# Layer normalisations inside the stages that follow them, and a mixture of experts in one block

## The reference

```python
def _layernorm(x, axis=-1, eps=1e-05):
    m = jnp.mean(x, axis=axis, keepdims=True)
    v = jnp.var(x, axis=axis, keepdims=True)
    return (x - m) / jnp.sqrt(v + eps)
...
    x = x + _L1_xattn_ref(_layernorm(x, axis=-1), ctx_2048, ctx_2048, L1_xattn_gamma)
    x = x + _L1_ffn_ref(_layernorm(x, axis=-1), ...)
    x = x + _L2_attn_ref(_layernorm(x, axis=-1), ...)
    x = x + _L2_xattn_ref(_layernorm(x, axis=-1), ctx_2048)
    x = x + _L2_ffn_ref(_layernorm(x, axis=-1), ...)
    x = x + _L3_attn_ref(_layernorm(x, axis=-1), ...)
    x = x + _L3_xattn_ref(4, 256, 256, L3_xattn_w, L3_xattn_u, _layernorm(x, axis=-1), ctx_2048)
    x = x + _L3_ffn_ref(_layernorm(x, axis=-1), ...)
```

## Time and profile before

| | us |
|---|---|
| median of 3 runs | 1465.18 |
| lowest and highest run | 1462.57, 1465.30 |
| profiled execution: its time | 1461.6 |
| profiled execution: its span, first to last instruction | 1459.9 |
| TensorE busy in the span | 1221.0 (84%) |
| VectorE, ScalarE, GpSimd busy | 794.9, 510.2, 319.6 |
| mean granted TensorE clock | 0.893 of full speed |

### The profile page before, as it was taken

One profiled execution on the slowest core, in us unless ns is written; L12 is line 12 of the kernel. 1 busy time (PEld: TensorE's weight loads), 2 busy tenths in 40 slices (PEclk: granted clock), 3 DMA queues, 4 the chain that ended last, 5 costly groups with the idle time before them and its releaser, 6 DMA issues. The chain is left out here.

```text
span 1459.9 us, 22518 instructions
## 1 busy us (share of the span) xinstructions
PE 1221.0 (84%) x8843; PEld 755.3 (52%) x8850; DVE 794.9 (54%) x2082; ACT 510.2 (35%) x934; POOL 319.6 (22%) x351
## 2 busy tenths in 40 slices
PE   3768679797958799779995997999999978985597
PEld 1335464465734554456663554555555545653354
DVE  2886757207577444657865665343111135767944
ACT  1018325313515433445444455111111114445443
POOL 0215402200002200135540221232222213440000
PEclk9878879898969599879996997999999987897799
DMA  9000000000040020000000000123233200000000
GB/s 367 1 0 2 1 1 2 0 0 1 0 188 1 8 109 0 1 1 3 3 2 0 2 2 1 49 62 101 80 97 90 87 15 1 2 2 0 1 1 29
DMA packets 13160, 47.95 MB, mean 33 GB/s; under 512 B 1640, under 2 KB 4712, under 8 KB 12288
## 3 DMA queue, kind: packets, MB, share of 16 engines
q1 hardware_dynamic: 13056, 46.53, 9.4%
HBM read 45.37 MB, written 1.15 MB: 32 GB/s over the span
## 5 line engine op out<-in xcount | busy, mean ns | idle before, releaser
L744 ACT ACTIVATE PT<-PS 128x384 f32<-128x384 f32 (+1 forms) x320 | 153.2, 531 | 214.0 <-PE PS L583 156.4
L1786 PE MATMUL PS<-HT,WA 128*128 128x512 f32 x448 | 201.4, 593 | 1.4 <-DVE MO L1854 1.4
L1854 DVE TENSOR_TENSOR MO<-PS,AO 128x512 f32<-128x512 f32 x56 | 38.7, 691 | 205.7 <-ACT AO L1844 205.6
L1786 PEld LDWEIGHTS PS<-HT,WA 128*128 128x128 f32 x448 | 84.7, 190 | 86.8 <-issue 82.9
L1844 ACT ACTIVATE AO<-PS 128x512 f32<-128x512 f32 x56 | 33.4, 597 | 252.1 <-PE PS L1786 252.1
L685 DVE CUSTOM_DVE_ANT_0 junk<-PS,TRI 128x128 bf16<-128x128 f32 (+1 forms) x384 | 113.0, 353 | 10.5 <-PE PS L564 7.0
L564 PE MATMUL PS<-KS,QM 32*128 32x128 f32 (+1 forms) x768 | 95.8, 383 | 19.5 <-PEq L897 8.7
L1794 PE MATMUL PS<-WA,HO 128*128 128x256 f32 x448 | 105.5, 378 | 0.0
L1794 PEld LDWEIGHTS PS<-WA,HO 128*128 128x128 f32 x448 | 84.5, 189 | 34.7 <-issue 24.9
L1908 POOL TENSOR_TENSOR HO<-MO,GR 128x512 f32<-128x512 f32 x44 | 57.9, 1316 | 168.6 <-PE PS L1794 168.6
L564 PEld LDWEIGHTS PS<-KS,QM 32*128 32x128 f32 x768 | 72.3, 206 | 42.9 <-issue 20.1
(11 more groups left out here) (314 smaller groups left out, 2390.4 us busy)
## 6 DMA issues: line engine op xcount, KB each, us to landing
WA<-w2f_in SPq DMA_DIRECT2D x28, 384.0 KB, 4.5
WA<-wl_in SPq DMA_DIRECT2D x1, 5137.0 KB, 15.8
GR<-gate_rows SPq DMA_DIRECT2D x20, 256.0 KB, 3.9
GB<-gate_rows SPq DMA_DIRECT2D x8, 512.0 KB, 7.6
WA<-wa_in SPq DMA_DIRECT2D x2, 1792.0 KB, 11.6
WB<-wb_in SPq DMA_DIRECT2D x1, 3208.0 KB, 18.5
WA<-wa_in SPq DMA_DIRECT2D x1, 2560.0 KB, 17.5
GR<-gate_rows SPq DMA_DIRECT2D x4, 448.0 KB, 3.8
```

The lines of the kernel that those rows point to most:

```text
L744: act.activation(PT[:, g % 3, st_slot(k), 0:W], PS[:, st_bank(g, k), 0:W], ACT.Exp, scale=scale).then_inc(S["at_exp"], 1)
L1786: last = pe.matmul(PS[:, 2 * c + half, :], chunk(i, half)[:, k * P:(k + 1) * P], HT[:, k, c * CH:(c + 1) * CH], start=k == 0, stop=k == KD ...
```

## The change

A new function `norm_steps` returns the steps of a normalisation for each engine instead of a block. Seven stages call it and put the steps at the head of their own lists, so that seven blocks go. TensorE's steps are spread in the stage: it turns two groups, waits for the copies of the groups that its first product reads (`columns`, a new semaphore `ht`), and turns the third and fourth group after the first products. VectorE and ScalarE go through all of their steps before the stage's own. `project_paired` takes the pieces by halves of the tokens (queries, keys, queries, keys, two each). `wkv_scan` runs its small preparations ahead of the normalisation and starts each batch's scan when that batch is copied. In `norm_steps` the splitting into parts is interleaved with the groups.

```diff
@@ -881,25 +903,35 @@
-    def project_paired(w, hd, V, spread, arrived=None):
-
-
-        d = dict(done)
+    def project_paired(w, hd, V, spread, arrived=None, **norm_of):
+
+
         cos = cst(f"cos{hd}", 1)
         sin = cst(f"sin{hd}", 1)
         nchunk = CH // T
-        work = [(w[a], a == "q", j, c) for a in ("q", "k") for j in range(2) for c in range(NCH)]
+        work = [(w[a], a == "q", j, c) for c in range(NCH) for a in ("q", "k") for j in range(2)]
...
+            norm = norm_steps(st, X, H, to_HT, tbank=lambda g: 4 + g, **norm_of)
...
+                    norm["turn"](pe, 0)
+                    norm["turn"](pe, 1)
                     for n, (a, _, j, c) in enumerate(work):
+
+                        if n == 0:
+                            norm["columns"](pe, 1)
+                        if n in (1, 2):
+                            norm["turn"](pe, n + 1)
+                        if n == 4:
+                            norm["columns"](pe, 3)
...
+                    norm["vector"](dve)
...
+                    norm["scalar"](act)
```

```diff
                     def go_up(i, c):
+                        if i == 0:
+                            norm["turn"](pe, 2 * c)
+                            norm["turn"](pe, 2 * c + 1)
+                            norm["columns"](pe, 2 * c + 1)
```

`experts1` becomes one block. The shared expert is the first slice and not the last, four core tiles come before the turns of the gates and four behind, the two bias rows are added to each other once and then to `X` in one pass, and ScalarE's Gelu of the biases stands first:

```diff
+        work = [(f, c) for f in (NF, *range(NF)) for c in range(NCH)]
+        EARLY = 4
...
+                def _(sp):
+                    sp.wait_ge(S["gates_copied"], d["gates_copied"] + 1)
+                    sp.dma_start(gate_rows[0:E, :], GT[0:E, :]).then_inc(S["gates_sent"], 16)
...
+                    go_up(0)
+                    go_up(1)
+                    pe.wait_ge(S["core_gelu"], 1)
+                    for t in range(EARLY):
+                        core(t)
+
                     pe.wait_ge(S["gates"], d["gates"] + 1)
                     for t in range(TT):
...
+                    for t in range(EARLY, TT):
+                        core(t)
+                    for n in range(NWK):
+                        if n + 2 < NWK:
+                            go_up(n + 2)
+                        go_down(n)
...
+                def _(act):
+                    act.activation(gb1[:], vv("b1"), ACT.Gelu).then_inc(S["bias_gelu"], 1)
+                    norm["scalar"](act)
...
+                    pool.tensor_tensor(bsum[:], rv("b_up1"), rv("b_core"), ALU.add).then_inc(S["row_sum"], 1)
+                    norm["tokens"](pool, TT // 2 - 1)
...
+                    dve.wait_ge(S["row_added"], 1)
+                    for t in range(EARLY):
+                        add(t)
                     dve.wait_ge(S["turned"], d["turned"] + 1)
...
+                    for t in range(EARLY, TT):
+                        add(t)
```

The scan and the ternary MLP:

```diff
                     def gaps(b):
+                        norm["columns"](dve, b)
...
                     dve.wait_ge(S["dve_chain"], d["dve_chain"] + 5)
+                    norm["vector"](dve)
                     gaps(0)
...
+        def vector(dve):
+            for g in range(G + 4):
+                if g < G:
+                    measure(dve, g)
+                if 1 <= g <= G:
+                    apply(dve, g - 1)
+                if parts is not None and 3 <= g < G + 3:
+                    rest_of(dve, g - 3)
+                if parts is not None and g >= 4:
+                    third(dve, g - 4)
...
+                        if i == 0:
+                            norm["columns"](pe, 2 * c + 1)
...
+                    norm["tensor"](pe)
                     for c in range(NCH):
                         go_up(0, c)
```

More of the change, by code:

```diff
@@ L310, in second @@
-                    def second(g):
-                        act.wait_ge(S["part_rest"], g + 1)
-                        act.activation(split(1, g), rest(g), ACT.Copy).then_inc(S["part_second"], 1)
-                    for g in range(NG + 2):
-                        if g < NG:
-                            root(g)
-                        if copies is not None and 1 <= g <= NG:
-                            copies(act, g - 1)
-                        if g >= 2 and dstT is not None:
-                            copy(g - 2)
-                        if g >= 3 and parts is not None:
-                            second(g - 3)
@@ L323, in _ @@
-                    if parts is not None:
-                        second(NG - 1)
+                    norm["scalar"](act)
                 if dstT is not None or rows is not None:
@@ L1138, in turn_context_and_weights, with mlp @@
         done["turned"] += CTX + 8
-    def mlp(n, up, down, bias):
-        d = dict(done)
+    def mlp(n, up, down, bias, **norm_of):
         tag = str(nc.next_id())
@@ L1496, in mixing, with experts1 @@
             done["moments"] += 3 * TT
-    def route(E, weights, logits_of, gates_of, G, GT, beside):
+    def experts1():
+        E = E1
+        NF = sum(FB1)
         tag = str(nc.next_id())
-        d = dict(done)
+        owner = [e for e in range(E1) for _ in range(FB1[e])]
+        work = [(f, c) for f in (NF, *range(NF)) for c in range(NCH)]
+        NWK = len(work)
+        EARLY = 4
         with ExitStack() as st:
@@ L1562, in route @@
[L1562 to L1583 removed]
+            GT, GH, MT = (tmp(x, [P, B * T]) for x in ("GT", "GH", "MT"))
@@ L1626, in gelus @@
-            def gelus(act):
-                act.activation(gb1[:], vv("b1"), ACT.Gelu).then_inc(S["bias_gelu"], 1)
-                for c in range(NCH):
-                    act.wait_ge(S["narrow"], c + 1)
-                    act.activation(GH[:, c * CH:(c + 1) * CH], PS[:, 3 + 4 * c, :], ACT.Gelu, bias=vv("b_down1"))
-                act.activation(GX, HT[:], ACT.Gelu)
-            route(E1, wB("router", KD), logits_of, gates_of, G, GT, beside=(biases, narrow, gelus))
+            bsum = tmp("bsum", [P, D])
@@ L1913, in experts2, with wkv_scan @@
                 done[name] += k
-    def wkv_scan():
-        d = dict(done)
+    def wkv_scan(left, pre, rows):
         tag = str(nc.next_id())
@@ L2056, in _ @@
                     turn(B - 1)
+            left.close()
             done["turned"] += B
-            done["dve_chain"] += 5
     def ternary():
@@ L2118, in ternary_mlp @@
             MP = tmp("MP3", [P, 3, NCH, CH], BF16)
+            norm = norm_steps(st, X, H, to_HT, parts=parts, tbank=lambda g: 4 + g)
+            d = dict(done)
             with nc.Block() as block:
```

441 lines of the change are left out of this document (227 added, 214 removed).

## The result

| | before | after |
|---|---|---|
| median, us | 1462.03 (6 runs) | 1451.81 (6 runs) |
| lowest and highest run | 1459.66, 1465.30 | 1447.40, 1453.40 |
| profiled execution: span | 1459.9 | 1451.2 |
| ratio of the times | | 0.9925, 95% interval 0.9910 to 0.9939 |

The changed kernel is faster by 0.75%, 11.0 us by the ratio (8.9 to 13.2); the forecast was 9.6. The median of before over six runs is 1462.0, 3 us under the median of three from which the forecast started, so the size of the gain is the fair comparison.

What follows compares the result with a forecast made beforehand. TensorE was taken to wait on a normalisation's latency, 68.6 us idle ahead of the turns. Seven seam terms summed to 9.6 us, taking the median from 1465.2 to 1455.6, written 1455.5; range 1450 to 1461.5.

Steps and rivals of the forecast that it cites:

- 1 MLP: First MLP: first Gelu starts as before, second product done about 0.7 us earlier; gain 0.7, ends 0 and 2.8.
- 2 mixture: First experts in one block: +0.2 us, ends -1.5 and +3; clock rising about 4.5 after sums, TensorE waiting 1.3 for gates.
- 3, 4 projection of layer 2 to second mixture: Layer 2's projection ends 1.8 us earlier, bound by ScalarE; second experts gain 0.9, VectorE's idle time covering later ScalarE sums.
- 5 projection of layer 3 with its attention: Layer 3's projection: TensorE binds, second copy 2.8 us earlier, two groups of turns (0.88) paid; gain 2.0, ends 0.3 and 2.8.
- 6 scan: Scan: first scan no longer behind two copies, the boundary and five small operations; gain 1.9 us, ends 1.5 and 2.2.
- 7 ternary MLP: Ternary MLP: first product starts about 1385.0 instead of 1387.16, one more subtraction ahead; gain 2.1 us, ends 1 and 2.8.
- Tails, not waits: Normalisations: waits of the first two groups of turns stay; of 68.6 us idle the change takes only the tails.
- First product 2.8 earlier: First MLP and both projections: TensorE's first product can start about 2.8 us earlier, behind the second copy.
- with that rise moved along: First MLP: the clock's rise shifts with the earlier product, so product 0 ends at 272.0 and the fourth copy at 273.7.
- ScalarE, not TensorE, sets the end: Layer 2's projection: ScalarE's list, starting behind the fourth copy, ends at 629.4 instead of 631.2; gain 1.8 us.
- Rival A: TensorE's clock does not move along with the earlier work; this or no effect at all, ending within 2.9 us, chance 0.08.
- Rival C: Slower: the mixture of short turns and pauses keeps TensorE's clock down; at 4.5 us per seam 1469; chance 0.04.

Runs made afterwards that it cites:

- run with later turns: Changed kernel with all eight core tiles, not four, ahead of the turns of the gates in the first mixture; 1456.15 us, ratio 0.9952 to before.
- run with the turns first: Changed kernel with, in both projections, the third group of turns ahead of the first product and the fourth ahead of the first value tile; 1449.47 us, ratio 0.9909.
- late Gelu: Changed kernel with the Gelu of the biases in the first mixture moved back behind the first exponential; 1451.73 us, ratio 0.9922 to before.

## Why the prediction was right, and where not

The forecast of 9.6 us lies within the interval of the measured gain (8.9 to 13.2). By seam, the forecast and what the stages' lengths of both profiles of each kernel show:

| seam | forecast | measured |
|---|---|---|
| 1 MLP | 0.7 | -0.3 |
| 2 mixture | 0.2 | 1.9 to 2.3 |
| 3, 4 projection of layer 2 to second mixture | 2.7 | 3.3 to 3.9 |
| 5 projection of layer 3 with its attention | 2.0 | 3.1 |
| 6 scan | 1.9 | 2.1 |
| 7 ternary MLP | 2.1 | 1.9 |
| sum | 9.6 | 12.1 to 13.0 |

The stages gained 2.5 to 3.4 us more than the sum of the terms, most of it in the mixture and in the two projections with the stretches behind them, while the MLP gave 1.0 less; that the medians come within 1.4 us of the forecast is in part luck.

1. *Tails, not waits.* Right. The turns' idle time stayed (67.2), one table load came, and running with the blocks apart gave the gain of the five later seams back.

2. *First product 2.8 earlier.* Right: 2.8 in the MLP and in both projections, and in the mixture the routing products start 1.4 earlier for a forecast of 1.3. What that is worth is the clock's and ScalarE's matter.

3. *MLP, 0.7.* The step that failed is "with that rise moved along". The clock rose 12.3 us after the stage's start before and 12.4 now, so the two groups of turns behind product 0 took 1.9 us at half clock for the forecast 0.9, and the fourth copy ended at 12.3 for the forecast 11.4. That the Gelu would bind was foreseen, and that end of the range was 0; the measured -0.3 lies just under it.

4. *Mixture, +0.2.* Two terms were wrong in the same direction. No run shows the 4.5 us from the end of the sums to the clock's rise: in the two profiles of the changed kernel it was 2.9 and 3.7 us (before, behind the first wide product of seams 1, 3, 5 and 7, 3.3, 5.7, 5.1 and 3.6). The clock was back 31.1 to 32.1 after the start for 32.9, the core tiles ended 39.5 to 40.0 for 40.4, and the gates were back at 43.2 to 43.4 for 45.0: about 1 us because their turns came earlier, the rest because the last leg took 4.2 and not 4.7. The wait of 1.3 us on TensorE did not come. The run with later turns shows that the picture was right and the margin nearly as thin: some 3.7 us later cost 3.5 to 3.8.

5. *Projection of layer 2 and second mixture.* The terms were 1.8 and 0.9. Among the kernels with the change two patterns of the clock occur, and the lengths move together: 34.2 to 34.6, 248.2 to 248.6, 312.0 to 312.1, or 34.7 to 35.1, 246.1 to 246.4, 313.3 to 313.4. Against before, the second pattern is 2.0, 1.0 and 0.85, the last one the term of seam 4 to the tenth. The first gains more in the second mixture (2.1, with 3.4 us less at half clock) and loses 1 us in the attention between. The first sums to 3.3 to 3.9, the second to 3.7 to 4.4. "ScalarE, not TensorE, sets the end" holds for the changed kernel, where its list waits 1.1 us behind the fourth copy as forecast; the run with the turns first shows that GpSimd's rotated pieces stand right behind it.

6. *Projection of layer 3.* 2.3 in the stage, for 2.0, and 0.8 more in the attention behind, which the forecast did not count. In the kernels with the clock's second pattern it is 1.6 to 1.9 and 0.5 to 0.6.

7. *Scan and ternary MLP.* The first scan starts right behind the last subtraction (compare), and the ternary product 10.8 after its stage's start for 12.7:

```profile
1319.38 0.74 DVE L283 TENSOR_SCALAR H<-X,mom,rstd 128x256 f32<-128x256 f32 x2
...
1320.04 1.27 DVE L1975 TENSOR_TENSOR_SCAN O<-VEC,HT 128x256 f32<-128x256 f32 x2
...
1378.47 1.89 PE L2171 MATMUL PS<-parts,WA 128*128 128x512 bf16 x4 [1.93 <-DVE parts L292]
```

Rival A, the clock that does not move along, was true of the MLP and of the late Gelu, and not of the seams behind: there the stages' clock rose (0.84 to 0.90 and 0.80 to 0.86 in the two projections; in that of layer 2 it was back 10.2 and 10.7 us after the start for 14.6 before). What work costs at half clock the changed kernel's projection of layer 2 shows: its first product took 3.78 us at 0.50 (from 603.05), its second, with as many rows, 1.88 at 1.00 (from 608.09). Rival C did not occur. Of the 5.5 us that its window shows TensorE busy, 3.7 are one-column sums and 1.9 the turns of the gates behind them. Taking the added table switch out moved the routing products by 1.4 us, about the 1.28 of the load and the 0.22 of the Gelu; nothing beyond these two shows.

## What to carry to other kernels

Put a latency's last steps (turns, copies) in front of the product that they would otherwise wait behind, when they are ready by then and something else waits for them (the MLP's stage took 64.00 for 66.66); where what is won there only meets the next wait, as in the projections (34.20 for 34.24 and 34.54), it makes no difference. Ask of each microsecond that an edit wins whether TensorE's granted clock is 1.00 at that point: ahead of the clock's return it may be spent at 0.50, where the projection's product took 3.78 us for 1.88. Small products behind which the clock falls belong where idle time or few wide products follow (the mixture took 116.74 with all forty sums ahead of the loop and 112.58 with half of them where TensorE waits for the core Gelu, one profile each). And measure edits by the length of their stage in the profile, where a repeat agreed to 0.3 us, while the head alone moved by 7. Take a second profile where the clock in the stage differs, since the same stage code came out 3 us apart in two kernels.

## What was not expected of the hardware

Forty one-column products in a row kept TensorE busy all the time in which they ran, and yet in every profile a half-clock stretch began in or right behind them, at either place in the program, 6.8 to 10.2 us long (3.4 in one profile, the one with all normalisations apart); with twenty in a row there was none the first time and 3.4 us the second. The clock's pattern is not free chance either: of identical stages, lengths mostly came again to 0.02 us or in one of two patterns, while the head of the program, identical in all kernels, moved over 7 us and the mixing stage over 2.5. What decides between the patterns stays open. So does why the MLP's clock came back 3.4 us earlier with all the turns ahead; an order with the same turns and other pauses would have told, and was not run.
